# A second wait for GpSimd's building of queries in the self attentions of a perceiver kernel

## The reference, cut to what matters

```python
# layer 0: 16 heads of 8, rotary queries and keys, tokens see their own page of 32 and earlier ones
scores = jnp.einsum('bqhd,bkhd->bhqk', q, k) * scale
scores = jnp.where(allowed[None, None], scores, jnp.finfo(scores.dtype).min)
attn = jax.nn.softmax(scores, axis=-1)
out = jnp.einsum('bhqk,bkhd->bqhd', attn, v).reshape(B, T, E)
return out @ wo
# layer 1: 16 heads of 8, a mask from the 16 tokens of highest importance of each item
scores = jnp.einsum('bhqd,bhkd->bhqk', q, k) / np.float32(np.sqrt(Dh))
m2 = sel[:, :, None] | sel[:, None, :]
w = jax.nn.softmax(jnp.where(m2[:, None, :, :], scores, -jnp.inf), axis=-1)
att = jnp.einsum('bhqk,bhkd->bhqd', w, v).transpose(0, 2, 1, 3).reshape(Bx, Sx, Dx)
return att @ Wo + bo
```

## Time and profile before

| | us |
|---|---|
| median of 3 runs | 2218.91 |
| lowest, highest | 2211.12, 2220.21 |
| the profiled execution, its own time | 2216.74 |
| its span in the profile | 2215.0 |
| TensorE (matmuls) busy | 1961.9 |
| VectorE busy | 1446.3 |
| ScalarE busy | 1271.1 |
| GpSimd busy | 208.9 |

### The profile page before, as it was taken

The page is one execution under the profiler, slowest core; times in us unless marked ns, Lnnn a source line. Parts: engine busy times, 40 slices in busy tenths (PEclk is TensorE's granted clock), DMA queues, the critical chain, the costliest instruction groups (busy, mean ns, idle before and its releaser), DMA issues. The chain is left out here.

```text
span 2215.0 us, 62661 instructions
## 1 busy us (share of the span) xinstructions
PE 1961.9 (89%) x27120; PEld 1200.7 (54%) x27120; DVE 1446.3 (65%) x2472; ACT 1271.1 (57%) x1799; POOL 208.9 (9%) x183
## 2 busy tenths in 40 slices
PE   8899999999898686999699999999999996668888
PEld 5577777777654443333355665655666653344333
DVE  3676777777535775555478878878788873376444
ACT  3476777777633452222278777787777775254222
POOL 4000000000201411111000000000000000040000
PEclk8899999999998578999799999999999998867999
DMA  3544454554101200111644545445545430210110
GB/s 136 119 126 124 129 134 130 131 134 122 40 0 29 30 2 20 39 35 31 133 76 85 90 91 92 84 93 93 94 86 89 92 47 1 39 22 1 38 29 29
DMA packets 63919, 161.46 MB, mean 73 GB/s; under 512 B 21796, under 2 KB 26020, under 8 KB 63268
## 3 DMA queue, kind: packets, MB, share of 16 engines
q1 hardware_dynamic: 63652, 157.53, 33.5%
HBM read 68.13 MB, written 1.05 MB: 31 GB/s over the span
## 5 line engine op out<-in xcount | busy, mean ns | idle before, releaser
L593 ACT ACTIVATE Pb<-ps 128x1024 f32<-128x1024 f32 (+2 forms) x640 | 633.7, 1001 | 207.8 <-PE ps L542 159.9
L647 DVE TENSOR_REDUCE MX<-ps 128x2 f32<-128x804 f32 (+1 forms) x386 | 368.6, 985 | 68.6 <-PE ps L509 67.5
L562 PE MATMUL ps<-Pb,V 128*17 128x64 f32 (+1 forms) x13312 | 360.6, 248 | 9.7 <-issue 4.5
L649 DVE TENSOR_REDUCE MX<-ps 128x1 f32<-128x402 f32 (+1 forms) x512 | 277.9, 570 | 108.9 <-PE ps L513 100.6
L562 PEld LDWEIGHTS ps<-Pb,V 128*17 128x17 f32 (+1 forms) x13312 | 256.3, 97 | 97.3 <-issue 64.6
L509 PE MATMUL ps<-KST,QW 50*128 50x402 bf16 (+1 forms) x1024 | 177.3, 342 | 31.3 <-ACT V L612 17.3
L542 PE MATMUL ps<-QW,KST 50*128 50x128 bf16 (+1 forms) x3328 | 166.0, 220 | 29.7 <-ACT Pb L593 29.2
L493 PE MATMUL ps<-W,CT 128*128 128x128 f32 (+1 forms) x1144 | 169.2, 287 | 0.0
L513 PE MATMUL ps<-KST,QW 96*128 96x402 bf16 (+1 forms) x512 | 155.7, 343 | 8.9 <-issue 4.9
L542 PEld LDWEIGHTS ps<-QW,KST 50*128 50x128 bf16 (+1 forms) x3328 | 101.5, 96 | 113.3 <-ACT Pb L593 83.5
L485 PE MATMUL ps<-CT,W 128*128 128x402 f32 (+1 forms) x352 | 146.2, 541 | 13.5 <-DMA CT<-ctxT 11.9
(11 more groups left out here) (239 smaller groups left out, 2759.9 us busy)
## 6 DMA issues: line engine op xcount, KB each, us to landing
CT<-ctxT SPq DMA_DIRECT2D x44, 800.5 KB, 4.8
KST<-HL SPq DMA_DIRECT2D x320, 100.1 KB, 3.0
KST<-C SPq DMA_DIRECT2D x320, 100.1 KB, 3.0
ABO<-ctxT SPq DMA_DIRECT2D x10, 800.5 KB, 5.1
T<-ctxT SPq DMA_DIRECT2D x10, 800.5 KB, 4.4
KST<-HL SPq DMA_DIRECT2D x128, 50.0 KB, 2.7
KST<-C SPq DMA_DIRECT2D x128, 50.0 KB, 2.7
CT<-experts SPq DMA_DIRECT2D x32, 192.0 KB, 2.3
```

Source lines behind the costliest of these rows:

```text
L562: mm = nc.tensor.matmul(ps[32 * quad:32 * quad + m, SUM, oc:oc + nh * S], V[0:n, b % 2, tile, v0:v0 + m], Pb[0:n, buffer(b, x), ti * att.W ...
L593: nc.scalar.activation(Pb[0:n, buffer(b, x), 0:banks * 512].rearrange("p (a c) -> p a c", a=banks), score_banks(b, x)[0:n, 0:banks, :], AC ...
L647: nc.vector.reduce_max(MX[:, b % 2, 2 * j:2 * j + 2], work(job)[:, :, 0:n], AX.X).then_inc(freed["dve"], 1)
L649: nc.vector.reduce_max(MX[:, b % 2, j:j + 1], work(job)[:, 0:n], AX.X).then_inc(freed["dve"], 1)
```

## The change

GpSimd's building of the queries of pair p waits, from p = 4 on, for `negm` to reach `before + p` as well as for the scores. `negm` counts the finished shifts, one for each pair, so `before + p` is the shift of pair p-1. Everything else stays.

```diff
             def pool_queries(p):
                 if p >= 4:
                     eng.wait_ge(scores, before + p - 3)
+                    eng.wait_ge(negm, before + p)
                 for u in range(2):
                     if before + p + u:
                         eng.wait_ge(qbuilt, 2 * before + 2 * p + u)
```

## The result

| | before | after |
|---|---|---|
| median of 7 runs, us | 2218.91 | 2232.27 |
| lowest, highest | 2206.98, 2222.12 | 2228.42, 2236.93 |
| the profiled execution, its span | 2216.74, 2215.0 | 2232.95, 2231.2 |

The ratio after to before is 1.0073, with a 95% interval of 1.0049 to 1.0097. The forecast was 2232 us, slower.

The account below looks back on a forecast made before the run. VectorE was taken to set the attention loop's 4.24 us period; the new wait's 4.78 us ring replaces it. Adding 6.1 and 7.9 us, 14.0 together, to 2218.91 gave 2232.9, stated as 2232 us; range 2223 to 2242 us.

Parts of the forecast that it names:

- The collision: L978 beside GpSimd's multiplications takes 1.06 us; the wait makes it 0.18, 0.88 us off VectorE's period.
- The ring: GpSimd, TensorE, VectorE and back once per pair: links sum to 4.78 us, the new period; chance 0.88.
- The upper bound of the ring: With 0.18 us for each of three pickups between engines, the ring comes to about 5.0 us.
- rival (3): Both attentions: long pickups, 5.0 us per round, and clock staying low; 20.8 us more, 2240 us; chance 0.13.
- The whole: First attention 6.1 us later, second 7.9 us later, together 14.0 us; 2232 us.
- about 55 us: Length given for each stretch in which a self attention runs.
- Rival (2): At GpSimd's new wait: shift found done already, or relief and ring balance; 2219 us; chance 0.07.
- relief: Attention loop: only the collision goes; 6.5 us less at low clock, at most 21 at high; chance 0.05.
- 3.97 us: TensorE's period at the low clock without the collision: 4.24 less its 0.27 us of waiting.
- 1.35: Time in us that GpSimd's two instructions would have to take, in place of 2.16, for the ring not to bind.
- 3.36 us: VectorE's own period without the collision, 4.24 - 0.88; the relief period at the high clock.
- The 0.5% bound: Whole kernel: what a measurement can tell from no change, 11 us; chances slower 0.71, same 0.26, faster 0.03.

Follow-up runs that it names:

- the first experiment: The kernel before with a second GpSimd wait, for the shift of pair p-2 in place of pair p-1: ratio 0.9902 (0.9864 to 0.994).
- the looser wait: The kernel before with a second GpSimd wait, for the shift of pair p-2: ratio 0.9902, and 0.991 when run again.
- The half-size run: The changed kernel, each multiplication from pair 4 on building only two of four groups of queries: ratio 0.9969 (0.9948 to 0.9989).
- The second comparison: The changed kernel again, beside the kernel before on one chip: ratio 1.0056 (1.0031 to 1.0081).
- e1_loose: The kernel before with a second GpSimd wait, for the shift of pair p-2: ratio 0.9902 (0.9864 to 0.994).
- e2_exp: The kernel before with a second GpSimd wait, for ScalarE's exponential of pair p-4: ratio 0.9931 (0.9904 to 0.9957).
- e3_five: The kernel before with query buffers for five pairs, GpSimd waiting for scores of pair p-5 and the shift of pair p-2: ratio 0.9901.
- e9_memset: The kernel before, GpSimd writing zeros twice in place of its two multiplications from pair 4 on: ratio 0.991 (0.9879 to 0.9942).
- e11_loose_again: The kernel before with the wait for the shift of pair p-2, timed again with more rounds: ratio 0.991 (0.9881 to 0.994).

## Why the prediction was right, and what in it was wrong

**The collision.** Right in size for most pairs, and in effect. Before, L978 took 0.90 to 1.07 us in 20 of the 32 pairs, and it takes 0.18 us in all of them now; no other VectorE instruction took the delay over. What the forecast didn't see is that at the high clock the collision wanders: in four pairs of the second attention the scores end earlier, GpSimd starts some 0.4 us ahead of L976, and L976, which also reads SBUF twice, is held in place of L978.

```profile
1966.09 2.19 POOL L994 TENSOR_TENSOR QW<-QS,HM 115x512 bf16<-115x512 bf16 x2 [1.48 <-PE ps L911]
1966.48 0.68 DVE L976 SCALAR_TENSOR_TENSOR MH<-MX 128x16 bf16<-128x16 f32 x1
...
1967.19 0.18 DVE L978 SCALAR_TENSOR_TENSOR MH<-MX,MH 128x16 bf16<-128x16 f32 x1
```

It costs 0.50 us there and not 0.88. The collisions of the first attention add up to 0.72 + 11 x 0.88 = 10.4 us, those of the second to 0.72 + 7 x 0.88 + 4 x 0.50 = 8.9 us.

**The ring.** Right, link by link. In the period shown above, with the forecast in brackets: GpSimd's two multiplications 2.15 us (2.16), to TensorE's load 0.06 (0.05), to the reduction 0.72 (0.68), to L976 1.38 (1.40), to L978 0.21 (0.21), L978 0.18 (0.18), to GpSimd 0.14 (0.10). The sum is 4.84 us; the forecast was 4.78. The link that the trace of before didn't show, from VectorE to GpSimd, was inside its bounds of 0.06 and 0.18 (0.15, if the cast is taken with the 0.69 us that it has by itself and not with half of the two). The 0.20 us less at the high clock are what was said of L884. Two more runs then moved the ring's longest member and the period followed it, 3.99 and 5.97 us beside 4.84, and in the kernel without the ring an added multiplication left the period where it was. The upper bound of the ring was added up wrongly: with 0.18 us for each of three pickups, in place of 0.05, 0.08 and 0.10, it is 4.78 + 0.31 = 5.09 us and not about 5.0, and rival (3) would be 22.8 us and 2242 us, which is still inside the range.

**The whole.** The forecast was 6.1 and 7.9 us for the two attentions, 14.0 together; measured are 6.7 and 7.5, 14.2. The long ring at the low clock had been taken for all rounds; 6 of 22 ran at the high clock, 0.20 us shorter each, which about made up for the 0.06 us that each round was longer. That the sum came out so near is in this part luck. The stretches called about 55 us long are 69.0 and 67.6 us from the first load to the last output; no term used the 55. The median moved by 13.4 us (16 us by the ratio).

**The step that was wrong** is the sentence on what GpSimd finds when the scores of pair p-4 are done. The forecast took the L978 at 757.99 for the shift of pair p-1. It is that of pair p-2; the shift of pair p-1 is made a whole period later. Further down the forecast counted rightly, where it moved GpSimd's pair 4 behind the shift of pair 3 at 744.55 and called the L978 at 741.16 that of pair 2, so the sum was not touched. Rival (2) was argued against from the same misread row, and the shift that the wait asks for comes still later than that. But the mistake hid the better kernel: whoever believes that the wait for pair p-1 sits right behind the collision doesn't see that it overshoots by a period, and that the wait for pair p-2 takes the collision away without closing a ring of one period. The expectation of the first experiment fell for the same reason.

**The rival "relief"** had the right mechanism and didn't happen here, since the ring was longer, as argued. Its price was wrong at the low clock: 3.97 us had been worked out as 4.24 less TensorE's one visible wait, and the looser wait runs at 3.73 us there (GpSimd's starts at 745.17, 748.90 and 752.63). The row behind this is that L884 no longer comes 1.1 us after the values' L874, as at 758.82 and 759.92 before, but runs into it.

```profile
745.61 0.50 PEld L874 LDWEIGHTS ps<-W,C 64*128 64x128 f32 x2 [0.40 <-issue]
...
745.92 0.80 PEld L884 LDWEIGHTS ps<-KST,QW 51*128 51x128 bf16 x16
```

The wait named in the trace, 0.27 us, was thus less than the 0.51 us that TensorE had to give. The bound that hung on the 3.97 us was wrong too: for the ring not to bind, GpSimd's two instructions would have had to take 3.73 - 2.68 = 1.05 us and not 1.35, with 2.68 us for the rest of the ring as measured. The half-size run, at 1.31 us, is faster than before, but its period is still the ring's.

The whole gain of the looser wait, 0.9 to 1.0% or 19 to 22 us by the medians, came out at the upper end that had been given to relief, 21 us, and not near its 6.5; it is also near the 19.3 us that the collisions add up to. At the high clock the forecast 3.36 us was exact: VectorE's own sum, from 766.11 to 769.53 once 3.42 us, elsewhere 3.36 (GpSimd at 769.84 and 773.19, 3.35 us apart).

**Chances.** The 0.5% bound lies at 11 us; the measured 13.4 is over it, with the interval from 11 to 22 us. The second comparison's interval, 1.0031 to 1.0081, reaches below it; that the change is slower both show, that it is slower by more than 0.5% only the first.

## What to carry to other kernels

Before adding a wait that is meant to move work out of another engine's way, number the iterations on both engines and find the loosest event that does it; an event of the iteration just before the consumer's can close a ring, and the ring's period is the plain sum of its links, with no overlap between them (here 4.84 us of seven links). If that sum is more than the present period, the relief is lost. Here the same wait with a count one lower was 1.4% faster than the change. The sign that something could be had was a tiny instruction that took six times as long as its twin of the same shape.

## What the runs showed of the hardware

A VectorE instruction of 0.18 us with two SBUF inputs that starts beside a running GpSimd multiplication of 1.04 us ends about 0.03 us behind it: it takes 1.06 us when it starts 0.01 us after the multiplication (757.99), 0.90 when 0.21 us after (741.16), 0.68 when 0.39 us after (1966.48). It is held by the multiplication beside which it starts, the first or the second, and not by both. Beside GpSimd memsets of 0.98 us each it isn't held at all. Casts from PSUM and an addition with one SBUF input run beside the multiplication at their usual 0.69 and 0.31 us.

The granted clock had not been expected to follow. Over the whole of the two attentions it is 0.79 and 0.88 with the looser wait (0.88 and 0.88 in its second profile), against 0.55 and 0.67 before. These are its rows for stretches of 50 us, to be held against the earlier trace rows:

```profile
740.00:790.00 50.00, 39.99 (x1188) 27.83 (x1182) 42.79 (x94) 38.39 (x59) 23.00 (x23) 0.84 0.01 3
1935.00:1985.00 50.00, 37.73 (x1140) 26.26 (x1140) 46.45 (x104) 37.28 (x57) 24.93 (x24) 0.89 0.01 3
```

TensorE is busy a smaller share of the time there, 40 of 50 us against 46, but does more: 1188 matmuls in 50 us against 941. The looser wait gains 9.5 us in the first attention (10.7 in its second profile) and 8.6 in the second, where the collisions were worth 10.4 and 8.9 us of VectorE's time. That the shorter period brings the clock up is only argued. The five profiles of e1_loose, e2_exp, e3_five, e9_memset and e11_loose_again, with few or no collisions and no ring of one period, have 0.79 to 0.88 over an attention, but the clock also moves without a change of the period: the first attention had 0.62 with the third multiplication and 0.55 in the kernel before, at the same 4.25 us, and the changed kernel, with its longer period, had 0.59.
